# Delta stage of a transformer layer chain on one Trainium2 core: the forward substitution is done wholly by VectorE, instead of three quarters on VectorE and one on GpSimd

## What is computed

```python
h = _rms(x, attn_norm_w)
q, k, v = (silu(silu(_causal_dwconv(h @ W.T, conv))) for each of the three)
q, k = _l2norm(q), _l2norm(k)          # 32 heads of 16
beta = sigmoid(h @ Wbeta.T)
def step(S, inp):                      # scan over the 32 time steps
    kt, qt, vt, bt = inp
    err = einsum('bhvk,bhk->bhv', S, kt) - vt
    S = S - bt[..., None, None] * err[..., None] * kt[..., None, :]
    o = einsum('bhvk,bhk->bhv', S, qt)
x = x + _rms(o, out_norm_w) @ Wout.T
```

## Time and profile before

| | before |
|---|---|
| three timed runs | 3254.93, 3256.35, 3263.09 us, median 3256.35 |
| the profiled execution | 3251.3 us, its span 3249.3 us |
| TensorE busy | 2897.0 us, 89% |
| VectorE busy | 1944.5 us, 60% |
| ScalarE busy | 1462.6 us, 45% |
| GpSimd busy | 1007.6 us, 31% |
| products of the substitution, VectorE | 265.3 us in 248 instructions |
| subtracts of the substitution, VectorE | 282.2 us in 248 instructions |
| products and subtracts, GpSimd | 252.1 and 271.7 us in 248 each |

### The profile page before, as it was taken

One profiled execution on the slowest core, in us unless ns is written; L12 is line 12 of the kernel. 1 busy time (PEld: TensorE's weight loads), 2 busy tenths in 40 slices (PEclk: granted clock), 3 DMA queues, 4 the chain that ended last, 5 costly groups with the idle time before them and its releaser, 6 DMA issues. The chain is left out here.

```text
span 3249.3 us, 65853 instructions
## 1 busy us (share of the span) xinstructions
PE 2897.0 (89%) x26552; PEld 1541.2 (47%) x26552; DVE 1944.5 (60%) x2956; ACT 1462.6 (45%) x2438; POOL 1007.6 (31%) x710
## 2 busy tenths in 40 slices
PE   6999999587899988999844999999999699999997
PEld 3444444244454444444423444444444366666665
DVE  3444444259977978779891444445442466666665
ACT  2222222376665766757612422222222366666665
POOL 0000000125725527255290000000000267777776
PEclk9999999788989989989866999999999899999999
DMA  6998898200000000000003132322200111111010
GB/s 241 334 336 309 301 332 271 87 14 1 2 27 8 22 28 2 27 9 21 15 15 119 56 117 78 104 91 91 98 33 27 63 36 39 39 39 39 33 42 30
DMA packets 126423, 290.19 MB, mean 89 GB/s; under 512 B 30496, under 2 KB 35360, under 8 KB 122112
## 3 DMA queue, kind: packets, MB, share of 16 engines
q1 hardware_dynamic: 122752, 261.91, 23.0%
q10 hardware_dynamic: 3456, 25.17, 2.3%
HBM read 245.02 MB, written 42.01 MB: 88 GB/s over the span
## 5 line engine op out<-in xcount | busy, mean ns | idle before, releaser
L803 POOL TENSOR_TENSOR b_tmp<-b_L,b_U 128x496 f32<-128x496 f32 (+30 forms) x248 | 252.1, 1017 | 558.6 <-ACT b_L L1040 539.8
L1984 POOL TENSOR_TENSOR d_zb<-d_za 128x1024 f32<-128x1024 f32 x32 | 75.3, 2353 | 1047.0 <-DVE d_za L2040 1047.0
L845 PE MATMUL b_e<-b_hT,b_wqkv 128*128 128x512 f32 x768 | 367.8, 615 | 3.9 <-DVE b_raw L1223 3.1
L1273 DVE TENSOR_TENSOR b_U<-b_U,b_tmp 128x1488 f32<-128x1488 f32 (+30 forms) x248 | 282.2, 1138 | 8.6
L1271 DVE TENSOR_TENSOR b_tmp<-b_L,b_U 128x1488 f32<-128x1488 f32 (+30 forms) x248 | 265.3, 1070 | 32.3 <-ACT b_L L1040 26.4
L805 POOL TENSOR_TENSOR b_U<-b_U,b_tmp 128x496 f32<-128x496 f32 (+30 forms) x248 | 271.7, 1096 | 19.4
L1493 PE MATMUL c_r<-c_hT,c_g_pair 128*128 128x512 f16 x1056 | 255.5, 394 | 13.1 <-DVE c_hT L1658 13.1
L1223 DVE SCALAR_TENSOR_TENSOR b_raw<-b_e,b_cw,b_raw 128x496 f32<-128x496 f32 (+2 forms) x288 | 204.3, 717 | 99.2 <-ACT b_raw L1057 90.9
L1667 DVE SCALAR_TENSOR_TENSOR c_av<-c_r,c_sg 128x512 f32<-128x512 f32 x88 | 60.8, 691 | 305.3 <-PE c_r L1493 248.1
L1493 PE MATMUL c_r<-c_hT,c_u_pair 128*128 128x512 f16 x1056 | 242.7, 379 | 0.0
L1493 PE MATMUL c_d<-c_d_pair,c_aT 128*128 128x512 f16 x1056 | 241.0, 379 | 0.0
(11 more groups left out here) (229 smaller groups left out, 5486.1 us busy)
## 6 DMA issues: line engine op xcount, KB each, us to landing
a_cT<-in_ctxT SPq DMA_DIRECT2D x128, 512.0 KB, 9.6
a_cn<-in_ctx SPq DMA_DIRECT2D x128, 512.0 KB, 8.6
a_x_ln<-in_x SPq DMA_DIRECT2D x8, 1024.0 KB, 15.7
a_cw<-in_ctx SPq DMA_DIRECT2D x128, 64.0 KB, 9.2
a_x_res<-in_x SPq DMA_DIRECT2D x32, 256.0 KB, 11.1
x<-a_x_out SPq DMA_DIRECT2D x32, 256.0 KB, 10.9
b_xg<-x SPq DMA_DIRECT2D x8, 1024.0 KB, 5.4
om<-b_hT SPq DMA_DIRECT2D x32, 256.0 KB, 2.0
```

The lines of the kernel that those rows point to most:

```text
L803: nc.gpsimd.tensor_tensor(tmp[:, QV, s + 1:S, :], lo, us, ALU.mult).then_inc(pool_prod, 1)
L845: mm = pe.matmul(p[:], w_qkv[:, i, n, c * P:(c + 1) * P], hT[:, n, :], start=(n == 0), stop=(n == DC - 1))
L1273: V.tensor_tensor(U[:, 0:QV, s + 1:S, :], U[:, 0:QV, s + 1:S, :], tmp[:, 0:QV, s + 1:S, :], ALU.subtract).then_inc(sub, 1)
L1984: nc.gpsimd.tensor_tensor(o[:, :, 0, :], a[:, :, 0, :], a[:, :, 1, :], ALU.add).then_inc(bf, 1)
```

## The change

GpSimd's `solve` goes, with its two semaphores, and so do the waits on them in TensorE's block (ahead of the transposes of U) and ScalarE's (ahead of the copies of L). VectorE's product and subtract now run over all four quarters in one instruction each, 64 n elements where there were 48 n. The number and the order of VectorE's instructions stay as they were. GpSimd has nothing left to do in the delta stage behind its setup.

```diff
-        pool_prod, pool_sub = sem("pool_prod"), sem("pool_sub")
         stored = sem("stored")
-        QV = 3
...
-            def solve(k):
-                U = Uq[k % 2]
-                for i in range(NV):
-                    R.used(pool, 0, f"{k}.V{i}")
-                for i in range(NL):
-                    R.used(pool, 0, f"{k}.L{i}")
-                for s in range(S - 1):
-                    n = S - 1 - s
-                    lo = Lr[:, s + 1:S, QV, s].unsqueeze(2).to_broadcast([P, n, HD])
-                    us = U[:, QV, s:s + 1, :].to_broadcast([P, n, HD])
-                    nc.gpsimd.tensor_tensor(tmp[:, QV, s + 1:S, :], lo, us, ALU.mult).then_inc(pool_prod, 1)
-                    pool.wait_ge(pool_prod, (S - 1) * k + s + 1)
-                    nc.gpsimd.tensor_tensor(U[:, QV, s + 1:S, :], U[:, QV, s + 1:S, :], tmp[:, QV, s + 1:S, :],
-                                            ALU.subtract).then_inc(pool_sub, 1)
-                    pool.wait_ge(pool_sub, (S - 1) * k + s + 1)
-
-            for k in range(NG):
-                solve(k)
...
                     pe.wait_ge(sub, (S - 1) * k)
-                    pe.wait_ge(pool_sub, (S - 1) * k)
...
                     act.wait_ge(prod, dead)
-                    act.wait_ge(pool_prod, dead)
...
-                lo = Lr[:, s + 1:S, 0:QV, s].rearrange("u t q -> u q t").unsqueeze(3).to_broadcast([P, QV, n, HD])
-                us = U[:, 0:QV, s:s + 1, :].to_broadcast([P, QV, n, HD])
-                V.tensor_tensor(tmp[:, 0:QV, s + 1:S, :], lo, us, ALU.mult).then_inc(prod, 1)
+                lo = Lr[:, s + 1:S, :, s].rearrange("u t q -> u q t").unsqueeze(3).to_broadcast([P, 4, n, HD])
+                us = U[:, :, s:s + 1, :].to_broadcast([P, 4, n, HD])
+                V.tensor_tensor(tmp[:, :, s + 1:S, :], lo, us, ALU.mult).then_inc(prod, 1)
                 dve.wait_ge(prod, (S - 1) * k + s + 1)
-                V.tensor_tensor(U[:, 0:QV, s + 1:S, :], U[:, 0:QV, s + 1:S, :], tmp[:, 0:QV, s + 1:S, :],
+                V.tensor_tensor(U[:, :, s + 1:S, :], U[:, :, s + 1:S, :], tmp[:, :, s + 1:S, :],
                                 ALU.subtract).then_inc(sub, 1)
```

## The result

The changed kernel took 3289.74 us (median of four, 3284.27 to 3294.86), the kernel before 3257.93 beside it. The ratio is 1.0096, 95% interval 1.0074 to 1.0117: 0.96% slower, or 31.8 us by the medians. The prediction was 3289.

A forecast was written before the change was run, and what follows sets the result against it. The prediction took the end of VectorE's substitution, tied to the next start, to bound the delta stage; 7.6 + 3.6 + 19.6 + 6.3 - 4.5 = 32.6 us of growth on the median 3256.35 gave 3289 us, range 3271 to 3304.

The forecast's parts named there:

- What bounds the kernel: Delta stage: the end of one substitution is tied to the next start, so VectorE's last 26 us lie on the path.
- the tail: Steps 12 to 30 of VectorE's substitution, on the path at group boundaries: 31.4 us for 25.1, +6.3.
- the head: VectorE's steps 0 to 11: +0.3 and +3.0 us, hidden in waits for TensorE in groups 1 to 6.
- Rival 2: VectorE becomes the bound throughout, groups 0 to 6 growing 9.6 us each: +63, 3319 us; chance 0.07.
- Rival 3: TensorE and ScalarE cover the longer steps 12 to 30 at inner boundaries: 3266 us, or 3281 in part; chance 0.08.
- The cost of an instruction: VectorE's products and subtracts: 1.042 ns an element plus 0.16 us fixed, giving 31.9, 12.7 and 31.4 us by step range.
- Rival 4: Shared port makes the quarter free on VectorE: steps 12 to 30 stay at 25 us, 3252 us in all; chance 0.04.
- The sum: Growth over the groups of the delta stage: 7.6 + 3.6 + 19.6 + 6.3 - 4.5 = 32.6 us.
- slack of the next beta matmul: How much later VectorE may end at a boundary for nothing: 2.7 us at k = 2, 1.4 at k = 3 to 6.
- rival 1: TensorE's clock falls at the boundaries: 0 to 1.7 us each, +10 on top, 3299 us; chance 0.11.
- signs that I had named: Right: TensorE's busy time unchanged, among others. Wrong: another instruction cost, groups growing beyond steps 12 to 30, beta matmuls slow everywhere.
- The removed waits: Waits on GpSimd ahead of the transposes of U and copies of L: removing them costs and frees nothing.

The follow-up runs named there:

- head3: Changed kernel with VectorE doing three quarters in steps 0 to 11, four from step 12, quarter 3's early steps left out: 3285.03 us, ratio 1.0092 to the kernel before.
- tail3: Changed kernel with VectorE doing four quarters in steps 0 to 11, three from step 12, quarter 3's later steps left out: 3241.28 us, ratio 0.9956 to the kernel before.
- all3: Changed kernel with VectorE doing three quarters in every step, quarter 3 left out altogether, GpSimd idle: 3236.99 us, ratio 0.9945 to the kernel before.
- fill2: Changed kernel with extra identity transposes on TensorE, 32 ahead of the transposes of U and 24 behind them: 3280.54 us, ratio 1.008 to the kernel before.

## Why the prediction was right

**What bounds the kernel.** Right, and shown from both sides: the tail alone (head3) costs the change's price, the head alone (tail3) nothing. Rival 2, VectorE as the bound throughout, falls with all3: 7 us less work in each inner group, and the same time from start to start. Rival 3, the tail covered, falls with TensorE's wait of 4 us for VectorE at every boundary.

**The cost of an instruction.** Right: 31.82, 12.60 and 31.32 us against 31.9, 12.7 and 31.4, and 2.22 for 1984 elements. Rival 4, the free quarter, falls with this. Its one true case, the last substitution, came out as worked: VectorE waited 2.12 us for the root at the reciprocal (I had said about 2), and the substitution took 80.0 us for 84.5, so -4.5.

**The sum.** k = 0 grew by 7.4 (7.6 predicted). k = 1 by 5.8 and k = 7 by -4.5. The sum books each tail at its boundary less the slack of the next beta matmul; read from start to start the same terms are 6.3, 3.6 and four times 4.9 for k = 1 to 6. Measured in the traces: 5.8, 5.7, 6.8, 6.9, 6.9 and 9.5. The first is 0.5 below. In the others the traces show about 2 more, and 4.6 more at k = 6, some 12 us in all. That is the term that was mis-sized: TensorE's clock, rival 1, which I took at 0 with a bound of 1.7 for a boundary. So of the signs that I had named, one of being wrong came: the beta matmuls ran slow at all six boundaries, 5.1 to 5.3 us. One of being right didn't: TensorE's busy time in a group was to be unchanged and grew by 3.3 at k = 2. And groups 3 to 6 grew by more than the tail of 6.3, though not by spreads that waited for the norms (head3).

The way from the beta matmul to the group's last spread was 95.2 to 95.8 us for k = 2 to 5 and is 97.1 to 97.7; at k = 6 it was 89.9 and is 94.5. The clock was lower there in two places. In the 10 us behind the start of the beta matmuls it was granted at 0.83, 1.00, 0.83, 1.00 and 1.00 for k = 2 to 6 before, and at 0.83 to 0.85 after. From 50 to 80 us behind that start, where outer products run in small matmuls of 32 by 32, it was 0.77, 0.66, 0.77, 0.66 and 0.83, and is four times 0.66 and then 0.72. For k = 6, before and after:

```profile
1549.76:1579.76 30.00, 25.87 (x689) 14.19 (x688) 23.20 (x26) 19.21 (x27) 11.19 (x20) 0.83 0.01 3
```

```profile
1585.70:1615.70 30.00, 26.15 (x625) 14.08 (x623) 27.44 (x28) 17.27 (x21) 0.00 (x0) 0.72 0.01 2
```

An estimate from these clocks, the drop times the length of the stretch, is 1.6 us in the first place and 3.3 in the second at k = 6, together 4.9 for the 4.6 measured; at k = 2 to 5 it gives 3.2, 1.7, 3.1 and 1.7 for about 2 each. This also answers my reason for 0, the same time from start to start with either length of the beta matmuls: in the kernel before, a group with slow beta matmuls (k = 2, 4) had the higher clock in the later stretch, and the other way round (k = 3, 5). The other reason, that k = 1 is no longer than k = 2, looked at a boundary whose beta matmuls already took 4.96 us, with gaps of 0.3 and 3.3 us, while the changed kernel has 4 us and then 1.8. Whether the change itself lowers the clock in the later stretch isn't shown: in all3 and tail3, without the longer tail, it lies between 0.66 and 0.89 there. And at k = 6 fill2, with 1.00 around the boundary, still took 136.8 us for 137.1, so the boundary's gaps don't explain that group.

In the medians the kernels differ by 31.8, and 32.6 was predicted. That the two agree so well is partly luck: by the traces the missing term is some 12 us, by the medians it is near nothing, and the changed kernel was profiled in its longest run, the kernel before in one below all its timed runs. fill2 leaves the same width, 0 to 10.

**The removed waits.** No run took them away alone, so that they cost and gave nothing is not shown by itself. It fits all3, which has neither the waits nor GpSimd's work: its inner groups take about the time of before.

## What to carry to other kernels

A helper engine that slows the main one while both work may still be worth its place, if the disturbed stretch is hidden and the stretch that it shortens is not: ask where in the loop the main engine's work lies on the path, not how much work it has. Here the quarter on GpSimd paid because it ran ahead beside VectorE's other work and was done when the tail came. At a boundary where several engines hand over, put work of the waiting engine that needs none of it ahead of the wait; this gave 31 us on the kernel before, as much as the change cost. And when a forecast sets a term to 0 because two groups take the same time, look whether two things have cancelled in them: here the clock at the boundary and the clock 50 us later.

## What the runs showed of the hardware

Both engines' fp32 products with two inputs in SBUF disturb each other: VectorE's 16 instructions of steps 0 to 7 took 24.5 us alone and 31.6 beside GpSimd, its 38 of the tail 25.0 and 29.1. Over a substitution in which both run to the end they gain nothing from each other: 84.5 us with three quarters and one, 80.0 with four on VectorE alone.

A gap of about 4 us on TensorE and a second of 1.8 behind it let the granted clock of the 18 us around fall to 0.72; the 16 transposes took 3.68 for 1.97 and the beta matmuls 5.2 for 3.6. With 1.5 us left of the first gap, a second one of 3.3 us still left the beta matmuls at 5.0; with gaps of 0.6 and 0.8 they took 3.62. The length of a gap alone doesn't decide it: behind a single gap of 2.8 us the kernel before had them at 3.62 three times (k = 3, 5, 6) and at 5.32 twice (k = 2, 4).
